# Ten tables or nine looked up by matmul in a DLRM interaction tower on one core

## The reference, cut to what matters

```python
e = jnp.stack([tbl_0[ids[:, 0]], ..., tbl_25[ids[:, 25]]], axis=1)       # 512 samples x 26 x 128
all_emb = jnp.concatenate([bottom_output[:, None, :], e], axis=1)         # 27 features of 128
gram = jnp.einsum('bfd,bgd->bfg', all_emb, all_emb)
z = gram[:, _TRIU_I, _TRIU_J]                                             # 351 pairs
h = jnp.concatenate([z, bottom_output], axis=1)                           # 479
h = jnp.maximum(h @ W_top1 + b_top1, 0.0)                                 # 512
h = jnp.maximum(h @ W_top2 + b_top2, 0.0)                                 # 256
y = h @ W_top3                                                            # 1
```

## Time and profile before

| | us |
|---|---|
| median of 3 runs | 119.45 (118.17 to 120.21) |
| the profiled execution, its own time | 119.29 |
| its span, first to last instruction | 117.5 |
| PE busy | 108.8 (93%) |
| PEld busy | 87.5 (74%) |
| POOL busy | 71.2 (61%) |
| DVE busy | 70.5 (60%) |
| ACT busy | 63.8 (54%) |

### The profile page before, as it was taken

One profiled execution on the slowest core, in us unless ns is written; L12 is line 12 of the kernel. 1 busy time (PEld: TensorE's weight loads), 2 busy tenths in 40 slices (PEclk: granted clock), 3 DMA queues, 4 the chain that ended last, 5 costly groups with the idle time before them and its releaser, 6 DMA issues.

```text
span 117.5 us, 2578 instructions
## 1 busy us (share of the span) xinstructions
PE 108.8 (93%) x1004; PEld 87.5 (74%) x1004; DVE 70.5 (60%) x75; ACT 63.8 (54%) x87; POOL 71.2 (61%) x73
## 2 busy tenths in 40 slices
PE   5899999999999999999998990999799999999892
PEld 5778676776868776776667980899799799797890
DVE  1669999999999999999952640024242422121021
ACT  3395899999999969687505342222334123212111
POOL 2667868777777777787867767767777002030000
PEclk9999999999999999999999998559999999999999
DMA  3999999999879879932111238427545612710000
GB/s 50 283 246 259 258 268 259 262 280 204 246 200 268 239 175 288 267 109 73 43 46 50 66 65 155 108 69 131 113 106 110 112 49 41 107 44 0 23 0 1
DMA packets 19914, 16.67 MB, mean 142 GB/s; under 512 B 13785, under 2 KB 15701, under 8 KB 19902
## 3 DMA queue, kind: packets, MB, share of 16 engines
q1 hardware_dynamic: 16707, 12.03, 42.3%
q0 software_dynamic: 2160, 4.30, 14.1%
q10 hardware_dynamic: 1035, 0.18, 1.0%
HBM read 15.01 MB, written 1.49 MB: 140 GB/s over the span
## 4 chain that ended last, share of the span: by engine, by line
POOL 45%; PE 32%; issue 12%; DMA 6%; POOLq 1%; ACT 1%; DVE 1%; ACTq 0%; DVEq 0%
POOL mixed_sb L336 45%; PE banks L443 10%; PE banks L481 9%; PE banks L488 6%; PE banks L475 3%; PE banks L425 3%; DMA mixed_sb<-in_mixed_table,mixed_rows_sb 2%; DMA starts_sb<-in_starts 2%; DMA pairs<-products_dram 1%; POOLq L340 1%; PE banks L495 1%; ACT hidden L666 1%; DVE hidden L608 0%; ACTq L322 0%; DVE mixed_rows_sb L644 0%
## 5 line engine op out<-in xcount | busy, mean ns | idle before, releaser
L336 POOL DMA_INDIRECT mixed_sb<-in_mixed_table,mixed_rows_sb x64 | 68.6, 1072 | 21.4 <-issue 19.2
L620 DVE TENSOR_SCALAR one_hot<-banks,starts_sb 125x1024 fp32r<-125x1024 f32 x34 | 41.7, 1276 | 1.6 <-PE banks L392 1.4
L413 PE MATMUL banks<-one_hot,high 125*128 125x512 f32 x68 | 28.9, 426 | 0.1
L415 PE MATMUL banks<-one_hot,low 125*128 125x512 f32 x68 | 27.0, 397 | 0.0
L413 PEld LDWEIGHTS banks<-one_hot,high 125*128 125x128 f32 x68 | 13.0, 192 | 8.6 <-issue 3.2
L443 PE MATMUL banks<-turned 128*56 128x52 f32 x512 | 17.3, 232 | 1.1 <-issue 0.7
L443 PEld LDWEIGHTS banks<-turned 128*56 128x56 f32 x512 | 16.1, 148 | 2.7 <-issue 2.4
L584 DVE COPY products<-banks 120x416 f32<-120x416 f32 (+1 forms) x9 | 7.4, 826 | 15.9 <-PE banks L443 13.6
L695 ACT COPY turned<-banks 128x512 f32<-128x512 f32 x10 | 10.7, 1068 | 8.1 <-PE banks L415 8.1
L666 ACT ACTIVATE hidden<-banks,b_sb 128x128 f32<-128x128 f32 x12 | 4.4, 368 | 19.4 <-PE banks L481 11.8
L415 PEld LDWEIGHTS banks<-one_hot,low 125*128 125x128 f32 x68 | 13.1, 192 | 2.1
(11 more groups left out here) (33 smaller groups left out, 88.3 us busy)
## 6 DMA issues: line engine op xcount, KB each, us to landing
raw<-in_tbl SPq DMA_DIRECT2D x6, 448.0 KB
lookup_ids_sb<-in_lookup_ids SPq DMA_DIRECT2D x10, 256.0 KB, 7.1
raw<-in_tbl SPq DMA_DIRECT2D x4, 560.0 KB
products_dram<-products SPq DMA_DIRECT2D x14, 91.0 KB
mixed_sb<-in_mixed_table,mixed_rows_sb POOLq DMA_INDIRECT x64, 6.4
pairs<-products_dram SPq DMA_DIRECT2D x15, 39.0 KB
w_sb<-in_w SPq DMA_DIRECT2D x2, 256.0 KB
w_sb<-in_w SPq DMA_DIRECT2D x1, 512.0 KB, 13.2
```

Source lines behind the costliest of these rows:

```text
L336: pool.indirect_dma_start(mixed_sb[:, n, :], None, mixed_table, bass.IndirectOffsetOnAxis(ap=mixed_rows_sb[:, n:n + 1], axis=0),).then_inc ...
L413: pe.matmul(lookup_ps[:, i % 2, :], high[0:TABLE_PARTS, i % 2, c, :], columns, start=(c == 0), stop=False)
L415: last = pe.matmul(lookup_ps[:, i % 2, :], low[0:TABLE_PARTS, i % 2, c, :], columns, start=False, stop=(c == CHUNKS_OF[i] - 1))
L620: dve.tensor_scalar(one_hot[0:TABLE_PARTS, n % ONE_HOT_RING:n % ONE_HOT_RING + ONCE, :], banks[0:TABLE_PARTS, first:last + 1, :], float(-c ...
```

## The change

One of the 1250-row tables leaves the lookups, which are nine now. It becomes a side table: POOL fetches its rows by one more gather per tile (four in all, ahead of the tile's other gathers), each for 128 samples; PE turns it alone as a group of one transpose. SP issues one more small transfer of ids at the start. There are 21 turns instead of 17, and a table (`TURNED_BY_LOOKUP`) says how many are done after which lookup; `LATE_ORDER` is written anew.

The `low` part of every table is made in two halves, each followed by the one-hot of one chunk; the `high` part of the first table is made in two halves, too, and PE waits for each half apart. The clearing of PSUM rows 32 to 63 at the start goes, and two of four matmuls after the id spread.

The products in DRAM lie by sample: 28 rows of 26 x 32 floats, 3328 bytes, stored as whole rows, and the loads pick 384 or 128 bytes out of a row. The last tile's products are made for single samples, 28 rows by 26 columns, on four groups of 32 columns of the array.

```diff
+SIDES = 1
-LOOKUP = BY_SIZE[:TABLES - MIXED_PER_SAMPLE]
-MIXED = BY_SIZE[len(LOOKUP):]
+LOOKUP = BY_SIZE[:TABLES - MIXED_PER_SAMPLE - SIDES]
+SIDE = BY_SIZE[len(LOOKUP):len(LOOKUP) + SIDES]
+MIXED = BY_SIZE[len(LOOKUP) + SIDES:]
...
-WARM_UPS = (8, 4)
+WARM_UPS = (8, 2)
...
+SINGLE_TILES = {TILES - 1}
...
-LATE_ORDER = "mmmm tm tm tm mm mm tmm oo tom o tom ooo to tmm oo ooo ooooooo"
+LATE_ORDER = "mmmmmmtmtmmmtomoomooottooomtomootomoottmmoooooo"
+
+TURNED_BY_LOOKUP = {1: 1, 2: 3, 3: 4, 4: 5, 5: 6, 6: 8, 7: 9, 8: 11}
...
-PAIR_LOADS = [(0, OTHERS * i, i, OTHERS, 3, PER_CHUNK, FEATURES) for i in range(PER_CHUNK)]
+PAIR_LOADS = [(0, OTHERS * i, 3 * i, OTHERS, 3, 1, FEATURES) for i in range(PER_CHUNK)]
...
-        pairs = sb("pairs", [P, PAIR_CHUNKS, BATCH])
+        pairs = sb("pairs", [P, TILES, QUAD, PAIR_CHUNKS, QUADS])
...
             for j in samples:
                 eng.dma_start(
-                    bass.AP(products_dram.tensor, start + j * n,
-                            [[OTHERS * width(p), SLOTS], [width(p), OTHERS], [1, n]]),
-                    products[sample_rows(j), t % 2, j % PAIR, :, quads]).then_inc(signal, 16)
+                    bass.AP(products_dram.tensor, (p * QUAD + j) * SAMPLE, [[ROW, SLOTS], [1, ROW]]),
+                    products[sample_rows(p, j), p % 2, 0 if p in SINGLE_TILES else j % PAIR, :, :].rearrange("r g q -> r (g q)")
+                ).then_inc(signal, 16)
...
-                eng.dma_start(pairs[part:part + rows, chunk:chunk + chunks, columns_of(p)],
-                              bass.AP(products_dram.tensor, start + row * width(p),
-                                      [[step * width(p), rows], [chunk_step * width(p), chunks], [1, width(p)]])
-                              ).then_inc(signal, 16)
+                eng.dma_start(
+                    pairs[part:part + rows, p, :, chunk:chunk + chunks, :].rearrange("r j c q -> r j (c q)"),
+                    bass.AP(products_dram.tensor, p * QUAD * SAMPLE + row * QUADS,
+                            [[step * QUADS, rows], [SAMPLE, QUAD], [1, chunks * QUADS]])
+                ).then_inc(signal, 16)
...
+            for t in range(TILES):
+                if t == 0:
+                    pool.wait_ge(side_ids_in, 16)
+                for i in range(SIDES):
                     pool.indirect_dma_start(
+                        side_sb[:, t, i, :], None, side_tables[i],
+                        bass.IndirectOffsetOnAxis(ap=side_ids_sb[:, t, i:i + 1], axis=0),
+                    ).then_inc(side_gathered[t], 16)
...
+            sp.dma_start(side_ids_sb[:].rearrange("p t i -> p (t i)"), side_ids).then_inc(side_ids_in, 16)
...
+                    for j in range(QUAD) if t in SINGLE_TILES else []:
+                        last = pe.matmul(product_ps[sample_rows(t, j), b % len(PRODUCT_BANKS), k, 0:OTHERS],
+                                         turned[:, t, q, j, :], turned[:, t, q, j, 1:FEATURES],
+                                         start=True, stop=True)
-                    for h in range(HALVES):
+                    for h in [] if t in SINGLE_TILES else range(HALVES):
...
-            pe.wait_ge(banks_cleared, 1)
...
-                make_one_hot(i, 0)
+                make_one_hot(i, 0, ONCE)
...
-                for c in range(ONCE, VECTOR_CHUNKS_OF[i], ONCE):
-                    make_one_hot(i, c)
+                for half, chunks in enumerate(halves_of(i)):
+
+                    dve.wait_ge(high_set, highs(i, half))
+                    dve.tensor_tensor(low[0:TABLE_PARTS, i % 2, chunks, :],
+                                      raw[0:TABLE_PARTS, i % RAW_RING, chunks, :],
+                                      high[0:TABLE_PARTS, i % 2, chunks, :].bitcast(F32), ALU.subtract
+                                      ).then_inc(low_set, 1)
+                    make_one_hot(i, ONCE + half, 1)
+                for c in range(ONCE + 2, VECTOR_CHUNKS_OF[i], ONCE):
+                    make_one_hot(i, c, ONCE)
...
-            dve.memset(banks[UNUSED_ROWS, PRODUCT_BANKS[0]:PRODUCT_BANKS[-1] + 1, :], 0.0
-                       ).then_inc(banks_cleared, 1)
```

More of the change, by code:

```diff
@@ L97 @@
 PAIR_CHUNKS = len(CHUNK_ROWS)
+assert PAIR_CHUNKS == 3
 CHUNK_START = [sum(CHUNK_ROWS[:c]) for c in range(PAIR_CHUNKS + 1)]
@@ L113, in quads_of, with group_of @@
     return slice(first * GATHER_QUADS, (first + GATHERS_OF[b]) * GATHER_QUADS)
+GROUPS = []
+for tile in range(TILES):
+    GROUPS.append(("side", tile))
+    GROUPS += [("block", b) for b in range(BLOCKS) if tile_of(b) == tile]
+def group_of(b):
+    return GROUPS.index(("block", b))
 def plan():
@@ L143 @@
 LAST_LOOKUP = PLAN.index(("lookup", len(LOOKUP) - 1))
-COPIER = [1 if PLAN.index(("turn", n)) <= LAST_LOOKUP else n % 2 for n in range(BLOCKS)]
+COPIER = [1 if PLAN.index(("turn", n)) <= LAST_LOOKUP else n % 2 for n in range(len(GROUPS))]
 def copies(n):
@@ L480, in add_pairs @@
                 for c, rows in enumerate(CHUNK_ROWS):
-                    last = pe.matmul(out(n), w1_sb[0:rows, c, h * P:(h + 1) * P], pairs[0:rows, c, columns_of(p)],
-                                     start=False, stop=(c == PAIR_CHUNKS - 1))
+                    last = pe.matmul(out(n).rearrange("h (j q) -> h j q", j=QUAD), w1_sb[0:rows, c, h * P:(h + 1) * P],
+                                     pairs[0:rows, p, :, c, :], start=False, stop=(c == PAIR_CHUNKS - 1))
                 return last
@@ L583, in keep @@
             quads = quads_of(b)
-            copy(products[:, t % 2, :, :, quads].rearrange("p j g q -> p q (j g)"),
+            if t in SINGLE_TILES:
+                copy(products[:, t % 2, 0, :, quads].rearrange("p g q -> p q g"),
+                     product_ps[0:PRODUCT_ROWS, b % len(PRODUCT_BANKS), 0:quads.stop - quads.start, 0:OTHERS]
+                     ).then_inc(kept[which], 1)
+                return
+            copy(products[0:HALF_END, t % 2, :, :, quads].rearrange("p j g q -> p q (j g)"),
                  product_ps[0:HALF_END, b % len(PRODUCT_BANKS), 0:quads.stop - quads.start, 0:PAIR * OTHERS]
@@ L755 @@
     mixed_ids = mixed_ids.transpose(3, 1, 4, 0, 2).reshape(P, GATHERS)
+    side_ids = ids[:, SIDE].reshape(TILES, P, SIDES).transpose(1, 0, 2).reshape(P, TILES * SIDES)
     lookup_ids = np.zeros((ID_ROWS, ID_COLUMNS), ids.dtype)
@@ L773 @@
         nc, arg("dense", np.asarray(inputs["r_bottom_output"]).T),
+        arg("side_ids", side_ids), [arg(f"tbl_{f}", tables[f]) for f in SIDE],
         arg("lookup_ids", lookup_ids), [arg(f"tbl_{f}", tables[f]) for f in LOOKUP],
```

125 lines of the change are left out of this document (74 added, 51 removed).

## The result

| | before | after |
|---|---|---|
| median of the runs, us | 119.83 (118.17 to 120.34, 4 runs) | 111.69 (110.83 to 114.07, 4 runs) |
| ratio, 95% interval | | 0.938 (0.922 to 0.953) |
| profiled execution, its own time / its span | 119.29 / 117.5 | 111.79 / 110.0 |

In two later sets, beside the experiments, the changed kernel had medians of 113.2 and 113.0 (six runs each, 110.9 to 116.5; the second set's ratio 0.950, 0.939 to 0.961). The ratios leave out runs over 1.5% above the fastest of their kernel; where too few are left, medians alone are given. The forecast was 111.0 us, within 107.5 to 116; all three medians lie in that range, the two later ones above the 109 to 112.5 that it called most likely.

The account below looks back on a forecast made before the run. PE in the lookups, the gather queue and ACT's late loads were taken as close limits. Last product at 94.6 plus a 14.55 tail gave a 109.2 span; 1.8 outside it made 111 us, range 107.5 to 116.

Parts of the forecast that it names:

- Start: Up to PE's first lookup: no PSUM clearing, half a subtraction to wait for, one more DMA; 1.0 us earlier (0.8 to 1.3).
- Lookups' end: End of PE's last lookup: 62.43 less 1.0 and 6.19, plus 0.5, 1.3 and 1.5, gives 58.5 us (57 to 60).
- The early wait: PE held after the third lookup until the 13th gather lands: 0 to 3 us, taken as 1.5.
- Gathers: POOL's queue of 68: 3 us of stretching, last starts at 90.3, lands at 93.1, allowing the last product at 94.4.
- First pairs: Loads of the first part's stored products: landed at 71.4, PE there at 71.8; stores 0.4 us each, landing 2.35.
- Single samples: Last tile's products as 256 smaller matmuls: 3.3 us, no difference from halves, bounds -0.5 and +3.4.
- Tail: From the last product to the end: six early outputs follow, the part is there in time, 14.55 us.
- the fixed cost per matmul: Rival: each single sample in the last tile takes 52 ns, the tile 6.7 us, the time 113.4; chance 0.20.
- The lower clock behind a wait: Rival: PE's waits near 66 to 72 us join and clock 0.50 follows; about 113.5 us; chance 0.16.
- The stretching: Rival: gathers begun inside DVE's subtractions still lose 8.1 us; last product 99.5, time 115.9; chance 0.06.
- Long store rows: Rival, slower than before: 3328-byte store rows land late, PE waits twice; 121.9 us at a landing of 8.5; chance 0.05.
- three limits close together: Claim that PE in the lookups, the gather queue and ACT's late loads of the last part bound the kernel closely together.

Follow-up runs that it names:

- the kernel with halves: Changed kernel with the last tile's products by halves again (56x52, 128 matmuls), not single samples (28x26, 256): 115.8 us, ratio to before 0.972.

## Why the prediction was right

The sum came out (span 109.2 forecast, 110.0 measured), in part by luck. PE came to the first pairs 2.3 us later than forecast (74.13 for 71.8). From there to the last product it took 21.21 us, as summed (93.0 less 71.8). What covered most of the delay were the 1.6 us that had been set on top of that sum, for waits of PE and gathers for each other: PE waited for no gather there. The mechanism, six outputs moved ahead while PE and the gathers keep up with them, and a tail that is as long as the six take, is as forecast.

- **Start.** PE's first lookup came 1.36 us earlier; 1.0 was taken, 0.8 to 1.3 allowed. The reason is half right. Before, no row shows PE waiting for the whole subtraction, which ended at 9.32: its warm-up matmuls lasted until 9.42, of which two of four have gone. After, it does wait for the half, 0.98 us.
- **Lookups' end: 60.29, not 58.5, and outside 57 to 60.** The early wait was sized right in sum (1.5; measured 0.7 for gathers and 0.8 for the copy of the side table's turn), but ACT, which was behind, was not named. Two terms were too small. For the clock there was none: it is 0.50 from 8.9 to 12.1 us, and the first table takes 5.60 us (8.03 to 13.63) where it took 4.53 with a slow beginning of its own. For what DVE is short of there was 0.5: the second table takes 5.64 for 4.57, 0.55 of it a wait for a one-hot, and PE waits 0.46 more in the last table.
- **Gathers.** The last one started at 88.83, not 90.3, for 1.6 us of stretching and not 3. The direction was right, by shorter stretches: every half was still met, most of them near its end. With 2.8 to land, gathers allowed the last product near 93; PE was the later one.
- **First pairs.** Stores at 0.41 us each and the loads at 0.38 were right, and the landing was 1.9 and not 2.35 (67.89 to 69.80). Yet PE waited 1.65 us where no wait of its own was forecast. Blocks were put at 0.2 us after the lookups; they begin 1.45 after them, behind the last turns and 0.73 us of idle. And the turns that were to hold PE on its way did not, since the gathers came early.
- **Last product: 95.34, not 94.6.**
- **Single samples: 3.0 us, where 3.3 was taken for either form.** Halves cost 3.9 in such single blocks, not 3.3. The 26 ns per record were counted in a window that ended inside a block (28 records by 83.80); from the start of that block to what follows it, 83.07 to 84.03, are 30 ns for each of its 32. So the change gives 0.8 us, by the case in which four run where two ran (2.8 us). The Trainium skill's rule (TensorEngine Tiling (Array Packing), section Instruction Overhead), from which an estimated 6.4 us came, is not borne out: 64 records took 0.60 to 0.93 us.
- **Tail: 14.66 for 14.55,** PE's resumption 7.12 us after the last product for 7.07.

Of the rivals, the fixed cost per matmul is out (64 records of the last tile take no longer than 32 halves). The lower clock behind a wait did come at the first pairs in some runs, not in the profile of the changed kernel. The stretching is what the kernel with whole low parts shows; 115.9 had been given for it, and its runs took 114.3 to 122.2. Long store rows landed in 1.9 us, and in 2.9 at most in the other profiles, so the slower side had nothing to stand on.

The rule under the forecast, three limits close together, is borne out: the table's move nearly alone took 1.03 of the time before, the layout alone 1.00, the order alone brought no gain; of the changed kernel, twelve outputs behind the last product cost 2 to 4 us, the old layout 8, whole low parts 3 by the fastest run and some 6 by the median. One thing is not shown: the halves alone in the old kernel were not run, so what they bring without the table's move is open. And the limits hang together more than the theory has it: with whole low parts the lookups ended later for one table less, in both kernels that had them so (64.8 and 65.0, where ten tables ended at 62.43), and late gathers held an early turn for 3.2 and 1.8 us there.

**Still open:** why the clock falls behind one wait and not another. At the first pairs, waits of 1.45, 1.62, 1.75, 2.96 and 4.56 us were followed by a lower clock, waits of 1.31, 1.57, 1.65, 2.22 and 2.67 were not. The length alone doesn't decide. Such a stretch cost 1.5 us in the kernel with halves; how much of the spread of the changed kernel (110.8 to 116.5) comes from stretches like it is not shown.

## What to carry to other kernels

Work out for every limit when it would let the last step go, and change what lies behind that step only together with what holds it: here the three parts tried alone (the table's move, the layout, the order) were worth nothing or a loss, and all together 6 to 7.5 us. Price a run of short instructions and a lone block apart, each from its start to what follows it. Wherever a wait is added or moved in such a schedule, add the clock behind it to the bounds, early in the program too.

## What the runs showed of the hardware

- A gather that began inside a two-input DVE subtraction ended at the soonest some 0.81 us after it (0.80 to 0.83), for the whole (1.22 us) and the half (0.68 us), in all 14 profiles; the only two exceptions began within 0.04 us of the subtraction's start. So one that begins in the last 0.13 us of a subtraction loses nothing, and a shorter subtraction shortens the stretch by what it is shorter. Every whole subtraction had a gather begin inside it (6.8 to 8.1 us lost), of the 18 halves 5 to 18 had, by the profile (0.6 to 2.4 us lost).
- Matmuls of 28x26 on four groups of 32 columns start 9 to 15 ns apart in blocks of 64, those of 56x52 on two groups 30 ns apart in blocks of 32. In a run of several hundred of the short ones (one profile) PE stood still for 0.9 to 1.9 us at a time, with 16 KB of instructions arriving every 3.75 us.
- A store of 28 rows of 3328 bytes took 0.41 us of SP, one of 728 pieces of 128 bytes 0.87. The last of the first part's four landed 1.75 to 2.9 us after its issue in the ten profiles of the new layout (1.9 after the change), and 2.2 to 3.4 in the four of the old.
